# Differential attention: two partial row sums joined by TensorE in four column groups instead of by GpSimd

## The chip, the cores and the metric

The kernel runs on one core of a Trainium2 chip. The metric is the device time of one execution in microseconds; the time before is the median of 3 runs. The engines are TensorE (PE, its weight loads PEld), VectorE (DVE), ScalarE (ACT), GpSimd (POOL) and SyncE (SP), which issues the DMAs.

## What is computed

The program is a small model of two layers on an image of 2 x 256 channels x 48 x 48, so N = 2304 positions. Only the first layer's differential attention matters here. For each of 2 batches and 8 heads it computes, cut from the reference:

```python
Q1, Q2 = (Q[..., :hd], Q[..., hd:])          # hd = 32
K1, K2 = (K[..., :hd], K[..., hd:])
attn1 = softmax(einsum('bhnd,bhmd->bhnm', Q1, K1) * scale, axis=-1)
attn2 = softmax(einsum('bhnd,bhmd->bhnm', Q2, K2) * scale, axis=-1)
out = einsum('bhnm,bhmd->bhnd', attn1 - lam * attn2, V)
```

The kernel does not form the softmax: it exponentiates the scores less their row maximum, multiplies with V, and divides by the row sums of the exponentials at the end. The change is about these row sums, two (j = 0 and 1, for the two softmaxes) for each query.

## The kernel before, in words

`differential_attention` is the second of six stages. Its work is cut into 96 chunks (`CHUNKS`: 16 heads, 6 chunks of `WIDE` = 384 queries each). A chunk goes over 18 key tiles (`STEPS`) of 128 keys; for each tile and each j, TensorE makes 128 x 384 scores in a PSUM bank of a ring of four (`score`, line 417), and ScalarE writes their exponentials into one of nine `probs` buffers of 128 x 2 x 384 (`exps`, line 507). The keys lie on the partitions, so a row sum is a sum over the partitions and over the 18 tiles.

The tiles are first added up element by element, in two running sums: `on_dve` names the tiles 3, 7, 11 and 15, which VectorE adds (`add_up`, line 610, three additions, the last into `sum_dve`); the other 14 (`on_pool`) are added by GpSimd (line 661, 13 additions, into `run_pool`). Then GpSimd adds the two (line 667) into `row_sum`. Of these, TensorE makes the sum over the partitions in `sums(q)` (lines 458 to 465): a product with a matrix of ones for each j, the first in the upper half of the PSUM bank's partitions and the second in the lower. `s_accp` counts GpSimd's additions (`NPOOL` = 14 a chunk, with the joining one), `s_accd` VectorE's (`ND` = 3); `s_ring` counts the filled banks of the ring and `s_taken` the emptied ones.

From there the sums go by ScalarE to `sums_sb` (`take_sums`, line 528), by DMA to HBM and back in a compact form (`invert_sums`), through a reciprocal on VectorE (line 618), by DMA spread over the partitions, and into the product that normalises the output (line 626).

TensorE's order is written out by hand, in steps of three key tiles, six a chunk (`BATCHES`). A step consists of the six scores of the next three tiles, five products for the row maxima of a later chunk (line 428, reduced by VectorE in line 587, out of three PSUM banks), and the PV batch: the product of three tiles of `probs` with V (line 453, two halves of 64 columns, twelve recorded matmuls). After step 4 of a chunk's six (counted from 0) come the row maxima's broadcast (line 436), after the PV batch of step 1 the sums of the chunk before (`SUMS_AT`). VectorE takes the maxima of the same step, and after them an addition in the steps 1, 3 and 5, the reciprocal in step 2 and the normalising product in step 4. A `probs` buffer is written anew for the tile nine further on, when its PV product and its addition are done. All of these are f32.

Of the kernel before, what the change touches and what calls it, by code (L numbers as in the profile page):

```python
# [9 lines left out]
ALU = mybir.AluOpType  # L10
ACT = mybir.ActivationFunctionType
AX = mybir.AxisListType

P = 128
# [224 lines left out]
def differential_attention(nc, qk_hi, qk_lo, v_rows, lambdas, ident, row_sums, row_factors, o_rows):  # L239
# [18 lines left out]
    SUMS_AT, ROWS_AT, COMPACT_AT, NORMAL_AT = 1, 4, 2, 4  # L258
    PIECES = (0,), (1,), (2, 3), (4,)
    SCALE = HD ** -0.5  # L260
    on_dve = [g for g in range(STEPS) if g % 4 == 3]
    on_pool = [g for g in range(STEPS) if g not in on_dve]
    ND, NPOOL = len(on_dve) - 1, len(on_pool)
    add_after = {1: 1, 3: 2, 5: 3}
    TOTAL = CHUNKS * BATCHES

    def span(q):

        return q % PER_HEAD * T, T
# [34 lines left out]
    with ExitStack() as ctx:  # L304
# [2 lines left out]
        qs = [[sb(f"qs{i}{j}", [ROWS + 1, N], F32R) for j in range(2)] for i in range(2)]  # L307
        vs = [sb(f"vs{i}", [P, NT, 2, VD]) for i in range(2)]
        probs = [sb(f"probs{i}", [P, 2, WIDE]) for i in range(PBUF)]
        run_pool, row_sum, run_dve, sum_dve = (sb(n, [P, 2, WIDE]) for n in ("run_pool", "row_sum", "run_dve", "sum_dve"))  # L310
        maxes = [sb(f"maxes{i}", [P, 2, WIDE // P, PARTS_OF_KEYS]) for i in range(2)]
        neg_max = [sb(f"neg_max{i}", [P, 2, WIDE // P], F32R) for i in range(NEGS)]
        out_sb = sb("out", [P, WIDE])
        sums_sb = sb("sums", [P, WIDE])
        compact = sb("compact", [P, 2 * WIDE // P])
        compact_inv = sb("compact_inv", [P, 2 * WIDE // P])
        recip = sb("recip", [P, WIDE])
# [25 lines left out]
        with nc.Block() as block:  # L343
            @block.sync
            def _(sp):
                qh = qk_hi.rearrange("b (h j d) n -> (b h) j d n", j=2, d=HD)
                ql = qk_lo.rearrange("b (h j d) n -> (b h) j d n", j=2, d=HD)
                v_tiles = v_rows.rearrange("(t p) c -> p t c", p=P)

                def load(n, pieces):  # L350
                    par, (b, h) = n % 2, divmod(n, H0)
                    for piece in pieces:
                        if piece == 4:
                            sp.dma_start(vs[par][:, :, 0, :], v_tiles[:, b * NT:(b + 1) * NT, h * VD:(h + 1) * VD]
                                         ).then_inc(s_ldv[par], 16)
                        else:
                            j, kind = piece // 2, piece % 2
                            dst, parts = ((qs, (qh, qh, ql)), (ks, (qh, ql, qh)))[kind]
                            for r, src in enumerate(parts):
                                sp.dma_start(dst[par][j][r * HD:(r + 1) * HD, :].bitcast(F32),  # L360
                                             src[b * 2 * H0 + kind * H0 + h, j, :, :]).then_inc(s_ld[par], 16)

                def invert_sums(q):
                    w = span(q)[1]
                    sums_of, factors_of = row_sums[0:2 * w], row_factors[0:2 * w]
                    sp.wait_ge(s_taken, slot["sum", q] + 1)
                    sp.dma_start(sums_of.rearrange("(j n) -> j n", j=2), sums_sb[0:P:VD, 0:w]).then_inc(s_sums, 16)
                    sp.wait_ge(s_sums, (q + 1) * 16)
                    sp.dma_start(compact[:, 0:2 * w // P], sums_of.rearrange("(a c) -> a c", c=2 * w // P)
                                 ).then_inc(s_compact, 16)  # L370
                    sp.wait_ge(s_inv, q + 1)
                    sp.dma_start(factors_of.rearrange("(a c) -> a c", c=2 * w // P), compact_inv[:, 0:2 * w // P]
                                 ).then_inc(s_factors, 16)
                    sp.wait_ge(s_factors, (q + 1) * 16)
                    for j in range(2):
                        sp.dma_start(recip[j * VD:(j + 1) * VD, 0:w],
                                     factors_of[j * w:(j + 1) * w].partition_broadcast(VD)).then_inc(s_recip, 16)

                def store(q):
                    sp.wait_ge(s_norm, q + 1)  # L380
                    sp.dma_start(o_rows[:, q // PER_HEAD + 1, queries(q)], normed[:, 0:span(q)[1]]).then_inc(s_st_o, 16)

                sp.dma_start(ident_sb[:], ident).then_inc(s_const, 16)
                load(0, range(5))
                for i, l in enumerate(lambdas):
                    sp.dma_start(lam_in[:, i, :], l.rearrange("h d -> (h d)").partition_broadcast(P)).then_inc(s_lamin, 16)
                for q in range(CHUNKS):
                    n, c = divmod(q, PER_HEAD)
                    if q > 0:
                        invert_sums(q - 1)  # L390
                        store(q - 1)
                    if c < len(PIECES) and n + 1 < HEADS:

                        sp.wait_ge(s_pv, q * BATCHES + 1)
                        load(n + 1, PIECES[c])
                invert_sums(CHUNKS - 1)
                store(CHUNKS - 1)
                sp.wait_ge(s_st_o, CHUNKS * 16)

            @block.tensor  # L400
            def _(pe):
                pe.wait_ge(s_ones, 9)
                pe.wait_ge(s_ident, 1)

                def free(at):
# [50 lines left out]
                    mm.then_inc(s_pv, 1)  # L456

                def sums(q):
                    w = span(q)[1]
                    bank = free(slot["sum", q])  # L460
                    pe.wait_ge(s_accp, (q + 1) * NPOOL)
                    for j in range(2):
                        mm = pe.matmul(bank[VD * j:VD * (j + 1), 0:w], ones[:], row_sum[:, j, 0:w],
                                       start=True, stop=True, tile_position=(0, VD * j))
                    mm.then_inc(s_ring, 1)

                def scores_and_maxes(e, us):
# [25 lines left out]
            def _(act):  # L493
# [29 lines left out]
                def take_sums(q):  # L523
                    at = slot["sum", q]
                    if q > 0:
                        act.wait_ge(s_sums, q * 16)
                    act.wait_ge(s_ring, at + 1)
                    act.activation(sums_sb[:, 0:span(q)[1]], ring[at % BANKS][:, 0:span(q)[1]], ACT.Copy
                                   ).then_inc(s_taken, 1)

                act.wait_ge(s_lam, 2)
                act.activation(lam_exp[:], lam_sum[:], ACT.Exp).then_inc(s_lamexp, 1)
# [15 lines left out]
            def _(dve):  # L548
# [12 lines left out]
                def lambdas_ready():  # L561
                    dve.wait_ge(s_lamin, 16 * 4)
                    step = Chain(dve, s_lam)
                    for i in range(2):
                        ins = dve.tensor_tensor(lam_prod[:, i, :], lam_in[:, 2 * i, :], lam_in[:, 2 * i + 1, :], ALU.mult)
                    step.link(ins)
                    step.link(dve.tensor_reduce(lam_sum[:], lam_prod[:].rearrange("p i (h d) -> p i h d", d=HD),
                                                AX.X, ALU.add))
                    dve.wait_ge(s_lamexp, 1)
                    step.link(dve.tensor_tensor(lam_diff[:], lam_exp[:, 1, :], lam_exp[:, 0, :], ALU.subtract))  # L570
                    dve.wait_ge(s_ones, 9)
                    for b in range(B):
                        ins = dve.tensor_scalar(neg_lam[:, b * H0:(b + 1) * H0], lam_diff[:], -LAMBDA_INIT, None, ALU.add)
                    step.link(ins)
# [25 lines left out]
                def add_up(q, i):  # L600
# [3 lines left out]
                        dve.wait_ge(s_accd, q * ND + i - 1)  # L604
                    if i == ND and q > 0:

                        dve.wait_ge(s_accp, q * NPOOL)
                    acc = probs[on_dve[0] % PBUF] if i == 1 else run_dve
                    to = sum_dve if i == ND else run_dve
                    dve.tensor_tensor(to[:, :, 0:w], acc[:, :, 0:w], probs[g % PBUF][:, :, 0:w], ALU.add  # L610
# [37 lines left out]

            @block.gpsimd
            def _(pool):  # L650
                pool.memset(row_sum[:], 1.0).then_inc(s_ones, 1)
                for q in range(CHUNKS):
                    w = span(q)[1]
                    for i, g in enumerate(on_pool):
                        if i == 0:
                            continue
                        pool.wait_ge(s_taken, slot["score", q * STEPS + g, 1] + 1)
                        if q * NPOOL + i > 1:
                            pool.wait_ge(s_accp, q * NPOOL + i - 1)
                        acc = probs[on_pool[0] % PBUF] if i == 1 else run_pool  # L660
                        pool.tensor_tensor(run_pool[:, :, 0:w], acc[:, :, 0:w], probs[g % PBUF][:, :, 0:w], ALU.add  # L661
                                           ).then_inc(s_accp, 1)
                    pool.wait_ge(s_accd, (q + 1) * ND)
                    pool.wait_ge(s_accp, (q + 1) * NPOOL - 1)
                    if q > 0:
                        pool.wait_ge(s_ring, slot["sum", q - 1] + 1)
                    pool.tensor_tensor(row_sum[:, :, 0:w], run_pool[:, :, 0:w], sum_dve[:, :, 0:w], ALU.add  # L667
                                       ).then_inc(s_accp, 1)


def run_stages(eng, order, stage):
# [1535 lines left out]
```

## Time and profile before

| | us |
|---|---|
| median of 3 runs | 5432.79 (5431.19 to 5434.96) |
| the profiled execution | 5433.69 |
| its span | 5432.0 |
| TensorE busy in the span | 4963.1 |
| GpSimd busy in the span | 3056.2 |
| VectorE busy in the span | 3509.2 |

The span reaches from the first recorded instruction to the last. Busy times are sums over stages with different limits, so the stage in question has to be read by itself: it runs from 228 us, where its first DMA is issued, to about 3115 us, where the next stage begins. "Idle before" an instruction is the time that its engine did nothing just ahead of it, and the name behind an arrow is what ended that time. A matmul's recorded time contains its way through the array; what two of them cost is read from their starts.

### The profile page before, as it was taken

What the parts mean: (1) busy time and instruction counts of PE and PEld (TensorE: products, weight loads), DVE (VectorE), ACT (ScalarE), POOL (GpSimd) and SP (SyncE); (2) the same over time, 40 slices, a digit from 0 to 9 for tenths busy, and PEclk for the clock granted to TensorE, in tenths of its full rate; (3) what the DMA queues carried; (4) which work ended last, traced back from release to release, by engine and by line L of the source; (5) the groups of instructions that cost most, each with busy time, mean ns of one, the idle gap of its engine ahead of it and who ended that gap; (6) DMA issues with size and microseconds to landing.
All of it is one profiled execution on the core that took longest, in us unless ns stands there. A gap on an engine that the chain in (4) does not pass through costs nothing. (4 is left out here: it accounts for less than half of the span.)

```text
span 5432.0 us, 66178 instructions
## 1 busy us (share of the span) xinstructions
PE 4963.1 (91%) x22836; PEld 3030.5 (56%) x22836; DVE 3509.2 (65%) x5195; ACT 2424.0 (45%) x5309; POOL 3056.2 (56%) x1603
## 2 busy tenths in 40 slices
PE   8799999999999999999999779699996989888799
PEld 4465555555555555555555334377773555555355
DVE  3478887888878787888788445555553444545484
ACT  3255555555555555555555412144442333333332
POOL 0089999999999999999999711066661000000000
PEclk9899999999999999999999879799998999999899
DMA  6611111111111111111110056522201000000101
GB/s 221 209 42 40 33 32 45 41 32 40 38 45 32 33 40 45 40 33 32 45 41 18 25 155 174 159 56 71 71 14 63 24 16 14 23 17 12 52 7 53
DMA packets 229686, 295.77 MB, mean 54 GB/s; under 512 B 83326, under 2 KB 212870, under 8 KB 221838
## 3 DMA queue, kind: packets, MB, share of 16 engines
q1 hardware_dynamic: 229392, 292.06, 19.4%
q8 instruction: 159, 2.61, 0.2%
q14 instruction: 135, 1.11, 0.1%
HBM read 178.11 MB, written 113.87 MB: 54 GB/s over the span
## 5 line engine op out<-in xcount | busy, mean ns | idle before, releaser
L661 POOL TENSOR_TENSOR diff_run_pool<-diff_run_pool,diff_probs 128x768 f32<-128x768 f32 x1152 | 2233.4, 1939 | 170.9 <-ACT diff_probs L507 6.1
L587 DVE TENSOR_REDUCE diff_maxes<-diff_max 128x1 f32<-128x512 f32 (+1 forms) x2880 | 1627.9, 628 | 541.0 <-PE diff_max L428 540.6
L507 ACT ACTIVATE diff_probs<-diff_ring 128x384 f32<-128x384 f32 x3456 | 1432.9, 496 | 887.3 <-PE diff_ring L417 607.7
L453 PE MATMUL diff_out_ps<-diff_probs,diff_vs 128*64 128x384 f32 x6912 | 1245.3, 496 | 0.0
L428 PE MATMUL diff_max<-diff_ks,diff_qs 96*128 96x512 f32 (+1 forms) x2880 | 1146.2, 400 | 31.0 <-DMA diff_ks<-qk_hi 29.3
L417 PE MATMUL diff_ring<-diff_qs,diff_ks 97*128 97x384 f32 x3456 | 995.9, 343 | 47.8 <-ACT diff_probs L507 46.7
L428 PEld LDWEIGHTS diff_max<-diff_ks,diff_qs 96*128 96x128 f32 x2880 | 547.0, 190 | 397.2 <-issue 369.5
L417 PEld LDWEIGHTS diff_ring<-diff_qs,diff_ks 97*128 97x128 f32 x3456 | 654.3, 190 | 181.1 <-ACT diff_probs L507 85.1
L453 PEld LDWEIGHTS diff_out_ps<-diff_probs,diff_vs 128*64 128x64 f32 x6912 | 445.7, 136 | 513.4 <-issue 288.5
L2044 POOL MEMSET ffn_before<- 128x128 f32 x1 | 0.2, 204 | 988.5 <-POOLq L63 988.5
L1376 POOL TENSOR_TENSOR causal_run_sum<-causal_run_sum,causal_probs 128x768 f32<-128x768 f32 (+2 forms) x208 | 340.6, 1637 | 74.6 <-ACT causal_probs L1250 52.6
L1308 DVE TENSOR_REDUCE causal_maxes<-causal_max 128x2 f32<-128x768 f32 (+2 forms) x252 | 219.9, 873 | 248.0 <-PE causal_max L1183 164.8
L1250 ACT ACTIVATE causal_probs<-causal_ring 128x384 f32<-128x384 f32 (+2 forms) x504 | 206.2, 459 | 193.4 <-PE causal_ring L1161 105.7
L661 POOL TENSOR_TENSOR diff_run_pool<-diff_probs 128x768 f32<-128x768 f32 x96 | 222.8, 2321 | 54.9 <-ACT diff_probs L507 41.2
L610 DVE TENSOR_TENSOR diff_run_dve<-diff_probs 128x768 f32<-128x768 f32 x96 | 234.3, 2441 | 10.5 <-ACT diff_probs L507 10.5
L1182 PE MATMUL causal_max<-causal_ka,causal_qa 128*128 128x384 f32 (+2 forms) x504 | 177.7, 353 | 35.6 <-DVE causal_ident_r L1302 34.4
L982 POOL TENSOR_TENSOR mid_o_in<-mid_o_one,mid_o_two 128x1536 f32<-128x1536 f32 x12 | 41.1, 3428 | 261.2 <-DMA mid_o_two<-o_rows 224.9
L1160 PE MATMUL causal_ring<-causal_qa,causal_ka 128*128 128x384 f32 (+2 forms) x504 | 182.2, 362 | 0.9 <-ACT causal_probs L1250 0.9
L667 POOL TENSOR_TENSOR diff_row_sum<-diff_run_pool,diff_sum_dve 128x768 f32<-128x768 f32 x96 | 174.4, 1817 | 14.3 <-DVE diff_sum_dve L610 1.7
L1719 DVE RECIPROCAL rec_rstd<-rec_std 128x384 f32<-128x384 f32 x36 | 91.9, 2553 | 118.7 <-ACT rec_std L1642 118.7
L1183 PE MATMUL causal_max<-causal_kb,causal_qb 96*128 96x384 f32 (+2 forms) x504 | 165.9, 329 | 0.0
L1207 PE MATMUL causal_out_ps<-causal_probs,causal_vs 128*64 128x384 f32 (+2 forms) x1008 | 165.5, 464 | 0.0
(229 smaller groups left out, 5940.5 us busy)
## 6 DMA issues: line engine op xcount, KB each, us to landing
qk_hi<-proj_hi SPq DMA_DIRECT2D x12, 1536.0 KB, 5.8
qk_lo<-proj_lo SPq DMA_DIRECT2D x12, 1536.0 KB, 9.6
diff_qs<-qk_hi SPq DMA_DIRECT2D x64, 288.0 KB, 4.4
diff_ks<-qk_hi SPq DMA_DIRECT2D x64, 288.0 KB, 6.0
diff_recip<-row_factors SPq DMA_DIRECT2D x192, 96.0 KB, 2.8
o_rows<-diff_normed SPq DMA_DIRECT2D x96, 192.0 KB, 1.9
v_rows<-proj_vst SPq DMA_DIRECT2D x12, 768.0 KB, 7.6
diff_qs<-qk_lo SPq DMA_DIRECT2D x32, 288.0 KB, 5.3
```

What stands on the lines that cost most here:

```text
L417: pe.matmul(bank[:, 0:span(q)[1]], ks[par][j][:, g * P:(g + 1) * P], qs[par][j][:, queries(q)], start=True, stop=True).then_inc(s_ring, 1)
L428: pe.matmul(max_ps[u % MAX_BANKS][:, 0:keys.stop - keys.start], qs[n % 2][j][0:ROWS, at:at + P], ks[n % 2][j][0:ROWS, keys], start=True, s ...
L453: mm = pe.matmul(out_ps[VD * j:VD * (j + 1), 0:w], vs[n % 2][:, g, j, :], probs[g % PBUF][:, j, 0:w], start=g == 0, stop=g == STEPS - 1, t ...
L507: act.activation(probs[g % PBUF][:, j, 0:w], ring[at % BANKS][:, 0:w], ACT.Exp, scale=SCALE).then_inc(s_taken, 1)
L587: dve.tensor_reduce(maxes[q % 2][:, j, s:s + 1, h], max_ps[u % MAX_BANKS][:, 0:w], AX.X, ALU.max).then_inc(s_red, 1)
L610: dve.tensor_tensor(to[:, :, 0:w], acc[:, :, 0:w], probs[g % PBUF][:, :, 0:w], ALU.add).then_inc(s_accd, 1)
L661: pool.tensor_tensor(run_pool[:, :, 0:w], acc[:, :, 0:w], probs[g % PBUF][:, :, 0:w], ALU.add).then_inc(s_accp, 1)
L1160: pe.matmul(bank[:, lo:T], ka[turn % 2][j][:, keys], qa[j][:, queries], start=True, stop=False)
L1182: pe.matmul(to[:, j, 0:n], qa[j][:, queries], ka[turn % 2][j][:, keys], start=True, stop=False)
L1250: act.activation(probs[tile % PBUF][:, j, lo:T], ring[at % BANKS][:, lo:T], ACT.Exp, scale=SCALE).then_inc(s_taken, 1)
L1308: dve.tensor_reduce(maxes[z % 2][:, :, s, k], max_ps[u % 2][:, :, 0:n], AX.X, ALU.max).then_inc(s_red, 1)
L1376: pool.tensor_tensor(acc[:, :, lo:T], acc[:, :, lo:T], probs[tile % PBUF][:, :, lo:T], ALU.add).then_inc(s_acc, 1)
```

## The change

GpSimd's joining addition is given up, with the tile `row_sum` and its memset. GpSimd's last addition writes `sum_pool` instead of `run_pool`, as VectorE's last writes `sum_dve`. TensorE's `sums(q)` takes both: for each of the two partial sums, each j and each half of the 384 queries it makes a product of 192 columns with a ones matrix of 32 columns, eight products in all; the four (j, half) go to four groups of 32 partitions of the same bank, and the second partial sum is accumulated onto the first. The bank then holds 192 columns in place of 384, and the copy to `sums_sb` and the DMA out of it change accordingly. TensorE waits for VectorE's last addition itself, and VectorE and GpSimd wait, before they write their partial sums again, for the sums of the chunk before.

```diff
-    ND, NPOOL = len(on_dve) - 1, len(on_pool)
+    ND, NPOOL = len(on_dve) - 1, len(on_pool) - 1
...
-                    sp.dma_start(sums_of.rearrange("(j n) -> j n", j=2), sums_sb[0:P:VD, 0:w]).then_inc(s_sums, 16)
+                    sp.dma_start(sums_of.rearrange("(r n) -> r n", r=P // QUAD), sums_sb[0:P:QUAD, 0:w // 2]
+                                 ).then_inc(s_sums, 16)
...
                 def sums(q):
-                    w = span(q)[1]
+                    w = span(q)[1] // 2
                     bank = free(slot["sum", q])
                     pe.wait_ge(s_accp, (q + 1) * NPOOL)
-                    for j in range(2):
-                        mm = pe.matmul(bank[VD * j:VD * (j + 1), 0:w], ones[:], row_sum[:, j, 0:w],
-                                       start=True, stop=True, tile_position=(0, VD * j))
+                    pe.wait_ge(s_accd, (q + 1) * ND)
+                    for part in (sum_pool, sum_dve):
+                        for j in range(2):
+                            for half in range(2):
+                                row = (2 * j + half) * QUAD
+                                mm = pe.matmul(bank[row:row + QUAD, 0:w], ones[:, 0:QUAD],
+                                               part[:, j, half * w:(half + 1) * w], start=part is sum_pool,
+                                               stop=part is sum_dve, tile_position=(0, row))
                     mm.then_inc(s_ring, 1)
...
-                    act.activation(sums_sb[:, 0:span(q)[1]], ring[at % BANKS][:, 0:span(q)[1]], ACT.Copy
-                                   ).then_inc(s_taken, 1)
+                    w = span(q)[1] // 2
+                    act.activation(sums_sb[:, 0:w], ring[at % BANKS][:, 0:w], ACT.Copy).then_inc(s_taken, 1)
...
                     if i == ND and q > 0:
 
-                        dve.wait_ge(s_accp, q * NPOOL)
+                        dve.wait_ge(s_ring, slot["sum", q - 1] + 1)
...
-                pool.memset(row_sum[:], 1.0).then_inc(s_ones, 1)
...
+                        if i == NPOOL and q > 0:
+
+                            pool.wait_ge(s_ring, slot["sum", q - 1] + 1)
                         acc = probs[on_pool[0] % PBUF] if i == 1 else run_pool
-                        pool.tensor_tensor(run_pool[:, :, 0:w], acc[:, :, 0:w], probs[g % PBUF][:, :, 0:w], ALU.add
+                        to = sum_pool if i == NPOOL else run_pool
+                        pool.tensor_tensor(to[:, :, 0:w], acc[:, :, 0:w], probs[g % PBUF][:, :, 0:w], ALU.add
                                            ).then_inc(s_accp, 1)
-                    pool.wait_ge(s_accd, (q + 1) * ND)
-                    pool.wait_ge(s_accp, (q + 1) * NPOOL - 1)
-                    if q > 0:
-                        pool.wait_ge(s_ring, slot["sum", q - 1] + 1)
-                    pool.tensor_tensor(row_sum[:, :, 0:w], run_pool[:, :, 0:w], sum_dve[:, :, 0:w], ALU.add
-                                       ).then_inc(s_accp, 1)
```

## Rows read from the trace of the kernel before

**Rows 1.** The page: GpSimd's busy tenths in 40 equal slices of the span.

```profile
POOL 0089999999999999999999711066661000000000
```

**Rows 2.** Groups of GpSimd's instructions, 500 to 3099 us: count, busy, mean ns, idle before.

```profile
L661 POOL TENSOR_TENSOR diff_run_pool<-diff_run_pool,diff_probs 128x768 f32<-128x768 f32 x1061 | 2054.6, 1937 | 152.1
L661 POOL TENSOR_TENSOR diff_run_pool<-diff_probs 128x768 f32<-128x768 f32 x88 | 207.7, 2360 | 12.6
L667 POOL TENSOR_TENSOR diff_row_sum<-diff_run_pool,diff_sum_dve 128x768 f32<-128x768 f32 x89 | 161.6, 1816 | 11.8
```

**Rows 3.** Who waited for whom, 504 to 3099 us: us in total, times, longest.

```profile
ACT diff_probs L507 <- POOL diff_run_pool L661: 85.9, 87, 1.3
...
PE diff_ring L463 <- POOL diff_row_sum L667: 59.5, 86, 2.2
PE diff_ring L417 <- ACT diff_probs L507: 46.4, 88, 0.8
```

**Rows 4.** TensorE in order of time, settled chunk: start us, us, [idle before <-releaser].

```profile
2009.01 2.16 PE L453 MATMUL diff_out_ps<-diff_probs,diff_vs 128*64 128x384 f32 x12
2011.85 0.87 PE L463 MATMUL diff_ring<-diff_row_sum,diff_ones 128*64 128x384 f32 x4 [0.68 <-POOL diff_row_sum L667]
...
2015.74 2.16 PE L453 MATMUL diff_out_ps<-diff_probs,diff_vs 128*64 128x384 f32 x12
```

**Rows 5.** TensorE in order of time, early chunks: their PV batches, sums, one wait.

```profile
306.43 2.16 PE L453 MATMUL diff_out_ps<-diff_probs,diff_vs 128*64 128x384 f32 x12
...
334.13 2.16 PE L453 MATMUL diff_out_ps<-diff_probs,diff_vs 128*64 128x384 f32 x12
...
338.53 2.16 PE L453 MATMUL diff_out_ps<-diff_probs,diff_vs 128*64 128x384 f32 x12
340.51 0.81 PE L463 MATMUL diff_ring<-diff_row_sum,diff_ones 128*64 128x384 f32 x4
...
343.60 2.16 PE L453 MATMUL diff_out_ps<-diff_probs,diff_vs 128*64 128x384 f32 x12
...
361.62 0.50 PE L428 MATMUL diff_max<-diff_ks,diff_qs 96*128 96x512 f32 x1 [0.22 <-DVE diff_maxes L587]
...
362.53 2.16 PE L453 MATMUL diff_out_ps<-diff_probs,diff_vs 128*64 128x384 f32 x12
...
476.06 2.16 PE L453 MATMUL diff_out_ps<-diff_probs,diff_vs 128*64 128x384 f32 x12
```

**Rows 6.** Line 667, the joins: count, duration ns min/median/max, first and last start.

```profile
L667 POOL TENSOR_TENSOR diff_row_sum<-diff_run_pool,diff_sum_dve x96: 1799/1811/2347, 304.0 to 3097.7; 128x768 f32<-128x768 f32 x96
```

**Rows 7.** TensorE's weight loads in order of time, end of a settled PV batch.

```profile
2001.24 0.14 PEld L453 LDWEIGHTS diff_out_ps<-diff_probs,diff_vs 128*64 128x64 f32 x2 [0.18 <-ACT diff_probs L507]
2001.57 0.14 PEld L453 LDWEIGHTS diff_out_ps<-diff_probs,diff_vs 128*64 128x64 f32 x2 [0.18 <-issue]
2002.31 0.19 PEld L428 LDWEIGHTS diff_max<-diff_ks,diff_qs 96*128 96x128 f32 x1 [0.60 <-issue]
```

**Rows 8.** The same view, first stage, f32 products of 512 columns, full width.

```profile
151.02 0.19 PEld L167 LDWEIGHTS proj_v<-proj_wv,proj_xn 128*128 128x128 f32 x1 [0.24 <-issue]
151.45 0.19 PEld L167 LDWEIGHTS proj_v<-proj_wv,proj_xn 128*128 128x128 f32 x1 [0.24 <-issue]
```

**Rows 9.** Line 610, VectorE's first and last additions of a chunk: as rows 6.

```profile
L610 DVE TENSOR_TENSOR diff_run_dve<-diff_probs x96: 947/2539/2601, 284.7 to 3067.6; 128x768 f32<-128x768 f32 x96
...
L610 DVE TENSOR_TENSOR diff_sum_dve<-diff_run_dve,diff_probs x96: 945/947/2583, 303.0 to 3084.3; 128x768 f32<-128x768 f32 x96
```

**Rows 10.** Line 661, GpSimd's additions: as rows 6.

```profile
L661 POOL TENSOR_TENSOR diff_run_pool<-diff_run_pool,diff_probs x1152: 1798/1828/2488, 272.0 to 3095.8; 128x768 f32<-128x768 f32 x192
L661 POOL TENSOR_TENSOR diff_run_pool<-diff_probs x96: 1809/2367/2371, 270.1 to 3071.2; 128x768 f32<-128x768 f32 x96
```

**Rows 11.** TensorE in order of time, last chunk: first PV batch, and the sums.

```profile
3062.42 2.16 PE L453 MATMUL diff_out_ps<-diff_probs,diff_vs 128*64 128x384 f32 x12
...
3099.68 1.55 PE L463 MATMUL diff_ring<-diff_row_sum,diff_ones 128*64 128x384 f32 x4 [10.91 <-POOL diff_row_sum L667]
```

More of the change, by code:

```diff
@@ L260, in differential_attention @@
     SCALE = HD ** -0.5
+    QUAD = 32
     on_dve = [g for g in range(STEPS) if g % 4 == 3]
     on_pool = [g for g in range(STEPS) if g not in on_dve]
-    ND, NPOOL = len(on_dve) - 1, len(on_pool)
+    ND, NPOOL = len(on_dve) - 1, len(on_pool) - 1
     add_after = {1: 1, 3: 2, 5: 3}
@@ L309, in differential_attention @@
         probs = [sb(f"probs{i}", [P, 2, WIDE]) for i in range(PBUF)]
-        run_pool, row_sum, run_dve, sum_dve = (sb(n, [P, 2, WIDE]) for n in ("run_pool", "row_sum", "run_dve", "sum_dve"))
+        run_pool, sum_pool, run_dve, sum_dve = (sb(n, [P, 2, WIDE]) for n in ("run_pool", "sum_pool", "run_dve", "sum_dve"))
         maxes = [sb(f"maxes{i}", [P, 2, WIDE // P, PARTS_OF_KEYS]) for i in range(2)]
@@ L313, in differential_attention @@
         out_sb = sb("out", [P, WIDE])
-        sums_sb = sb("sums", [P, WIDE])
+        sums_sb = sb("sums", [P, WIDE // 2])
         compact = sb("compact", [P, 2 * WIDE // P])
@@ L401, in _ @@
             def _(pe):
-                pe.wait_ge(s_ones, 9)
+                pe.wait_ge(s_ones, 8)
                 pe.wait_ge(s_ident, 1)
@@ L570, in lambdas_ready @@
                     step.link(dve.tensor_tensor(lam_diff[:], lam_exp[:, 1, :], lam_exp[:, 0, :], ALU.subtract))
-                    dve.wait_ge(s_ones, 9)
+                    dve.wait_ge(s_ones, 8)
                     for b in range(B):
```

## Prediction, made before the result was known

> **What bounds the kernel now.** I read the page first, for where GpSimd (POOL) is busy, then POOL's groups of instructions over the settled part of the differential stage, the list of waits there, and last TensorE's order of time, once in a settled query chunk and once in an early one. The change lies wholly in this stage, 96 chunks long; nothing outside it is touched.
>
> In the page's slices POOL stands at eight or nine tenths from the third slice to the twenty-third [rows 1]. The groups say that this is saturation: between 500 and 3099 us the three groups are busy 2054.6, 207.7 and 161.6 us and idle 152.1, 12.6 and 11.8 us before their instructions, together 2600 us for a stretch of 2599 us. The idle time is 0.143 us for each of 1238 instructions, with no releaser named: the engine's own step from one addition to the next, not a wait [rows 2]. So a chunk lasts as long as its 13 additions and the joining one: (3097.7 - 304.0) / 95 = 29.41 us [rows 6].
>
> TensorE is paced by this through two waits a chunk: the sums wait for the join (59.5 us in 86 times), and a score waits for ScalarE (46.4 us), which itself waits for a probs buffer that POOL has not yet added (85.9 us) [rows 3]. Both fall into one step of TensorE's six. In the settled chunk it takes 6.73 us from one PV batch to the next, 2009.01 to 2015.74 [rows 4]; the same step of an early chunk, where POOL's backlog is still small and the sums start without a wait, takes 5.07 us, 338.53 to 343.60 [rows 5]. The early stretch shows what TensorE does if POOL lets it: 27.70 us for the chunk from 306.43 to 334.13, 28.40 for the next (to 362.53), and (476.06 - 306.43) / 6 = 28.27 on average [rows 5]. This, 1.14 us under 29.41, is where a shorter POOL chain can lead, and not POOL's own saving of 1.96 us.
>
> **POOL loses the join.** It takes 1.816 us and its step 0.14 [rows 2]: 1.96 us a chunk. POOL's own need falls to 29.41 - 1.96 = 27.45 us. Its last addition now writes sum_pool instead of run_pool; the join, of the same shape and also to a third tile, ran no longer than the others (1.816 against 1.937 us on average), so I cost this at nothing, between -0.1 and +0.1 us. The two tests of `s_ring` that guard the partial sums, on POOL's last addition and on VectorE's (in place of `s_accp`), ask for the sums of the chunk before, done four steps earlier; the cover is some 15 us of other additions, and without it POOL and VectorE would stall until TensorE's step 1. The memset that goes ran ahead of the stage's first loads: nothing.
>
> **TensorE's sums change shape.** Before: two f32 products of 384 columns, recorded as four matmuls, two in each half of the array. The pairs are worth seeing: weight loads of the PV batch come two at a time, 0.32 us apart (2001.24, 2001.57) [rows 7], while in the first stage f32 matmuls over the full width come singly, 0.43 us apart for 512 columns, which is 0.32 for 384 [rows 8]. So the halves run side by side, and the sums take 2 x 0.32 = 0.64 us; the step with them is 5.07 us against a plain one of (27.70 - 2 x 5.07) / 4 = 4.39 (the step with the row maxima, the other long one, taken as equal), a difference of 0.68 [rows 5]. After: eight products of 192 columns, so sixteen matmuls of 0.16 us, in four groups of 32 columns. No row shows more than two groups at once. If all four run side by side, it is 4 x 0.16 = 0.64 us again; two at a time, 1.29; one at a time, 2.58. I take four, as the halves show no loss against the full width [rows 7, 8]. To this comes one more change of shape, from 64-column groups to 32: the last pair's matmul starts 0.32 us after its load at 2001.57, the next full-width load at 2002.31, 0.42 us later, thus 0.1 us over the 0.32 that it streams [rows 7]. New price 0.74 us, so TensorE's floor becomes 27.70 + 0.1 = 27.80 us; ends of the unknown -0.1 and +2.0.
>
> The Trainium skill (TensorE: Matmul & The Clock Gate, Measured speedup vs the span model) gives 2.38 times for three column groups, which is 79% of three. By that the four rounds would be some 0.81 us, an estimate, and the sum below 16 us smaller; no row here can tell.
>
> The added wait of TensorE for `s_accd` asks for an addition that ended a step before (POOL's join waited for it until now): nothing, and behind it would stand the next step's maxima. ScalarE's copy of 192 instead of 384 columns is shorter, the DMA of the sums has four rows of 768 bytes instead of two of 1536, and both lie under the next step's work; nothing, with 0 to +0.1 us for the chain of DMAs, which VectorE's reciprocal meets sooner.
>
> **What is late next.** With 27.45 against 27.80 us POOL is no longer the bound, but barely, so VectorE's collisions with it become visible. VectorE's additions take 0.95 us alone, yet 2.5 in the median of the first of a chunk and up to 2.6 of the last [rows 9], and POOL's go from 1.83 to 2.37 when they meet one [rows 10]: each waits until the other has ended. In the settled kernel this hides behind POOL's queue. In the early chunk it does not: the maxima follow late, TensorE waits for VectorE at 361.62, and the chunk is 0.70 us longer than the one before [rows 5]. The six early chunks carry 28.27 - 27.70 = 0.57 us of such stalls each. With POOL nearly caught up its first addition begins shortly before VectorE's last one wants the same port in every chunk, which I expect to cost 0.3 to 0.6 us; I take 0.5, so a chunk of 27.80 + 0.5 = 28.3 us.
>
> **The end of the stage.** In the last chunk TensorE ends its PV batches early and then stands 10.91 us for POOL's backlog; the sums start at 3099.68, 37.3 us after the chunk's first PV batch (3062.42) [rows 11]. Without backlog POOL's 13 additions, 13 x (1.83 + 0.14) = 25.6 us and 1 us of collisions, begin about 3 us ahead of that batch (an estimate: the second tile is scored a step earlier): 24 us, so 13 us less.
>
> **Sum.** From the first PV batch of the second chunk to that of the last were 3062.42 - 306.43 = 2756.0 us, 94 chunks of 29.32 [rows 5, 11]. 94 x 28.3 = 2660.2: 95.8 less, and 13 at the end: 109 us. The span of 5432.0 becomes 5323; the profiled execution took 1.7 us more than its span (5433.69) and 0.9 more than the median (5432.79), so I say 5324 us.
>
> **Rivals.** (a) *Two groups at a time*, or sixteen pairs of load and matmul that cannot be issued faster: 0.65 us more a chunk, 28.95: 94 x 0.37 + 13 = 48 us less, 5385. Against it stands that the halves lose nothing; for it that four streams were never tried.
>
> (b) *One group at a time, slower than before.* Sums of 2.58 + 0.1 instead of 0.68 put 2.0 us on TensorE's path: 29.70 without any collision, 30.3 with them. Between 36 - 13 = 23 and 92 - 13 = 79 us more; 5480 as the middle. It decides from a chunk of 29.32 + 13 / 94 = 29.46 us on, that is, from sums of 1.9 us with the collisions counted. The rows speak against it: the loads of one pair lie inside the streaming of the pair before, in all 128 rows [rows 7]. The Trainium skill (TensorE: Matmul & The Clock Gate, The mechanism) says that a weight load overlaps a running matmul only where the row group differs; here all groups have the same rows, and by that rule this rival would hold. The trace disagrees, with loads 0.32 us apart beside matmuls that stream 0.32 us.
>
> (c) *Collisions at two steps of every chunk* with 0.7 us each: 27.8 + 1.4 = 29.2, hence 11 + 13 = 24 us less, 5408. For it: three VectorE additions and one product a chunk meet a POOL that is 98% busy. Against it: the early chunks, as busy, averaged 0.57.
>
> (d) *The other side of the forecast*: POOL locks to the steps so that no addition collides, 27.9: 5286.
>
> **Chances.** Forecast 0.67 (its own range 5285 to 5355, chunks of 27.9 to 28.6 us), (a) 0.15, (b) 0.05, (c) 0.09, (d) 0.04. What a measurement of this kernel can tell from no change is some 0.2%, 11 us. The forecast, (a), (d) and most of (c) are faster by more: 0.92; the rest of (c) 0.03 the same; (b) 0.05 slower. The range 5284 to 5393 holds the forecast, (a) and half of (d).
>
> **What would show it.** POOL: 13 additions a chunk and gaps over 0.2 us, waiting for ScalarE. TensorE: no wait for POOL ahead of the sums; 16 matmuls in about 0.7 us, four starting together (if two by two, (a); spread over 2.5 us, (b)); step with sums near 5.15 us. A step longer by 0.3 to 0.7 us with TensorE waiting for VectorE's maxima would be the collisions; two of them a chunk, (c). The sums of the last chunk some 24 us after its first PV batch. The forecast is wrong if TensorE's chunk has another floor than 27.8 us, or POOL is still without gaps.

## The result and the profile after

The changed kernel takes 5338.88 us (median of 4 runs, 5333.89 to 5341.33), against 5433.88 us of the kernel before in the same sessions: 95 us less, a ratio of 0.9823 with a 95% interval from 0.9806 to 0.984. The profiled execution took 5341.33 us, its span 5339.6.

GpSimd is no longer full. The page's slices, to be laid beside [rows 1]:

```profile
POOL 0089889889899889988888511166670000000000
```

And GpSimd's groups from 500 to 3000 us (count, busy us, mean ns, idle before and what ended it), to be laid beside [rows 2]:

```profile
L671 POOL TENSOR_TENSOR diff_run_pool<-diff_run_pool,diff_probs 128x768 f32<-128x768 f32 x968 | 1925.5, 1989 | 211.5 <-ACT diff_probs L514 95.4 <-POOL diff_run_pool L671 3.5 <-ACT diff_qs L521 0.4
L671 POOL TENSOR_TENSOR diff_sum_pool<-diff_run_pool,diff_probs 128x768 f32<-128x768 f32 x87 | 162.6, 1869 | 12.1 <-issue 0.8
L671 POOL TENSOR_TENSOR diff_run_pool<-diff_probs 128x768 f32<-128x768 f32 x88 | 159.7, 1814 | 29.9 <-ACT diff_probs L514 20.3
```

The joining addition is gone, and the idle time now names a releaser: GpSimd waits for ScalarE's exponentials, 95.4 + 20.3 = 115.7 us in 88 chunks, 1.3 us a chunk. The whole list of waits counts 198 of them:

```profile
POOL diff_run_pool L671 <- ACT diff_probs L514: 115.7, 198, 1.1
DVE diff_compact_inv L625 <- DMA diff_compact<-row_sums: 60.7, 88, 4.3
```

Before, no wait of GpSimd's was named in [rows 2]. The second line, VectorE's reciprocal waiting for the DMA of the sums, is taken up below.

TensorE in order of time, from the last step of one chunk to the second of the next (start us, us, engine, line, operation), beside [rows 4, 5]:

```profile
1495.06 2.16 PE L455 MATMUL diff_out_ps<-diff_probs,diff_vs 128*64 128x384 f32 x12
...
1499.90 2.16 PE L455 MATMUL diff_out_ps<-diff_probs,diff_vs 128*64 128x384 f32 x12
...
1504.30 2.16 PE L455 MATMUL diff_out_ps<-diff_probs,diff_vs 128*64 128x384 f32 x12
1506.38 0.53 PE L469 MATMUL diff_ring<-diff_sum_pool,diff_ones 128*32 128x192 f32 x8
1506.73 0.51 PE L469 MATMUL diff_ring<-diff_sum_dve,diff_ones 128*32 128x192 f32 x8
1507.17 0.50 PE L430 MATMUL diff_max<-diff_ks,diff_qs 96*128 96x512 f32 x1
...
1509.49 2.16 PE L455 MATMUL diff_out_ps<-diff_probs,diff_vs 128*64 128x384 f32 x12
```

The step with the sums takes 1509.49 - 1504.30 = 5.19 us, without a wait ahead of the sums; in the settled kernel before it took 6.73 [rows 4]. The plain step from 1499.90 takes 4.40 us. The step across the chunk's border, 1495.06 to 1499.90, takes 4.84, which is 0.44 us too much; the experiments are about this. The new shape of the sums costs what was taken for it: the first eight matmuls are 0.35 us ahead of the next eight, so a round of four column groups takes 0.17 us.

TensorE's weight loads at the same place show the same (start us, us):

```profile
1506.38 0.16 PEld L469 LDWEIGHTS diff_ring<-diff_sum_pool,diff_ones 128*32 128x32 f32 x8 [0.60 <-issue]
1506.57 0.29 PEld L469 LDWEIGHTS diff_ring<-diff_sum_dve,diff_ones 128*32 128x32 f32 x8
```

Eight loads within 0.16 us, and eight more beside the matmuls that stream; with one group at a time, as in rival (b), they would have been spread over 2.6 us.

The end of the stage, beside [rows 11], TensorE's first PV batch of the last chunk and its sums:

```profile
2978.01 2.16 PE L455 MATMUL diff_out_ps<-diff_probs,diff_vs 128*64 128x384 f32 x12
...
3003.07 0.87 PE L469 MATMUL diff_ring<-diff_sum_pool,diff_ones 128*32 128x192 f32 x8 [4.41 <-issue]
```

So the last sums start 3099.68 - 3003.07 = 96.6 us earlier. This splits into 94 chunks of (2978.01 - 304.92) / 94 = 28.44 us in place of 29.32, which is 83 us (304.92 is the first PV batch of the second chunk, 306.43 before [rows 5]: 1.5 us); and an end of 25.1 us in place of 37.3, 12 us. The span is shorter by 92.4 us only; by the first and last instructions of each stage, most of the difference lies in the second attention stage, which the change does not touch: 617.0 us in the profile before, 619.9 in this one. In the profiles below it is 616.8 to 617.1 in four and 619.9 in three, so it does not follow the edits.

### The profile page after: what moved, and what is told of

It is laid out like the page before. It is cut to its first block and busy times, and to the rows that moved or that the text cites. A ratio compares the mean times of both kernels' runs of the same rounds, so it can differ in the third digit from the quotient of the medians.

```text
span 5339.6 us, 68289 instructions
## 1 busy us (share of the span) xinstructions
PE 4968.2 (93%) x23988; PEld 3051.7 (57%) x23988; DVE 3456.5 (65%) x5195; ACT 2365.5 (44%) x5309; POOL 2878.0 (54%) x1506
## 5 line engine op out<-in xcount | busy, mean ns | idle before, releaser
L671 POOL TENSOR_TENSOR diff_run_pool<-diff_run_pool,diff_probs 128x768 f32<-128x768 f32 x1056 | 2099.6, 1988 | 233.7 <-ACT diff_probs L514 107.2
L514 ACT ACTIVATE diff_probs<-diff_ring 128x384 f32<-128x384 f32 x3456 | 1389.4, 508 | 846.8 <-PE diff_ring L419 805.0
L430 PE MATMUL diff_max<-diff_ks,diff_qs 96*128 96x512 f32 (+1 forms) x2880 | 1164.5, 406 | 42.1 <-DMA diff_ks<-qk_hi 29.4
L671 POOL TENSOR_TENSOR diff_run_pool<-diff_probs 128x768 f32<-128x768 f32 x96 | 174.2, 1814 | 302.3 <-ACT diff_probs L514 292.0
L617 DVE TENSOR_TENSOR diff_sum_dve<-diff_run_dve,diff_probs 128x768 f32<-128x768 f32 x96 | 212.8, 2217 | 0.0
L671 POOL TENSOR_TENSOR diff_sum_pool<-diff_run_pool,diff_probs 128x768 f32<-128x768 f32 x96 | 179.4, 1869 | 13.3 <-issue 0.8
L1165 PE MATMUL causal_ring<-causal_qb,causal_kb 97*128 97x384 f32 (+2 forms) x504 | 166.1, 330 | 0.0
```

The costliest lines, as they stand in the source:

```text
L430: pe.matmul(max_ps[u % MAX_BANKS][:, 0:keys.stop - keys.start], qs[n % 2][j][0:ROWS, at:at + P], ks[n % 2][j][0:ROWS, keys], start=True, s ...
L514: act.activation(probs[g % PBUF][:, j, 0:w], ring[at % BANKS][:, 0:w], ACT.Exp, scale=SCALE).then_inc(s_taken, 1)
L671: pool.tensor_tensor(to[:, :, 0:w], acc[:, :, 0:w], probs[g % PBUF][:, :, 0:w], ALU.add).then_inc(s_accp, 1)
```

## The experiments

Each kernel is the changed one with the edit shown. The ratios are to the kernel before as it ran beside each of them (medians 5432.98 us for e1 to e4, 5434.04 for e5 to e7). The mean chunk is read from the first PV batches of the second chunk and of the last, 94 chunks apart.

| kernel | median us | ratio to before (95%) | these two batches, us | mean chunk, us |
|---|---|---|---|---|
| before | 5433.88 | | 306.43, 3062.42 | 29.32 |
| changed | 5338.88 | 0.9823 (0.9806 to 0.9840) | 304.92, 2978.01 | 28.44 |
| e1, idle join | 5422.74 | 0.9983 (0.9973 to 0.9992) | 305.33, 3053.90 | 29.24 |
| e2, two groups | 5386.27 | 0.9918 (0.9901 to 0.9934) | 305.29, 3025.42 | 28.94 |
| e3, third addition later | 5310.41 | 0.9776 (0.9760 to 0.9792) | 304.26, 2946.05 | 28.10 |
| e4, scaling earlier | 5327.95 | 0.9810 (0.9794 to 0.9826) | 303.25, 2965.81 | 28.33 |
| e5, half the idle join | 5347.27 | 0.9839 (0.9823 to 0.9855) | 306.18, 2987.69 | 28.53 |
| e6, first addition waits | 5297.08 | 0.9750 (0.9733 to 0.9766) | 304.52, 2938.06 | 28.02 |
| e7, e6 with e4 | 5280.69 | 0.9718 (0.9701 to 0.9734) | 306.21, 2926.53 | 27.88 |

**e1. Was it GpSimd's time, or TensorE's wait for its result?** An addition of the join's shape comes back, and nobody reads it.

```diff
-    ND, NPOOL = len(on_dve) - 1, len(on_pool) - 1
+    ND, NPOOL = len(on_dve) - 1, len(on_pool)
...
-                    pe.wait_ge(s_accp, (q + 1) * NPOOL)
+                    pe.wait_ge(s_accp, (q + 1) * NPOOL - 1)
...
+                    pool.wait_ge(s_accp, (q + 1) * NPOOL - 1)
+                    pool.tensor_tensor(extra[:, :, 0:w], run_pool[:, :, 0:w], sum_pool[:, :, 0:w], ALU.add
+                                       ).then_inc(s_accp, 1)
```

> The changed kernel, with one GpSimd addition of the join's shape put back at the end of each chunk (run_pool + sum_pool into a tile that nobody reads); TensorE does not wait for it and sums as in the changed kernel. Theory (GpSimd's chain of additions was the bound): GpSimd needs 27.45 + 1.96 = 29.4 us a chunk again, is without gaps, and the time goes back to about 5430 us (before: 5433.9); TensorE again meets waits through ScalarE for probs buffers. Rival (what cost time was TensorE's wait for the join's result, not GpSimd's time): nobody waits for this addition, so the chunk stays near the changed kernel's 28.44 us and the time near 5339 us.

It goes back to 5422.74 us, with a chunk of 29.24. GpSimd's groups from 500 to 3050 us, and one line of its list of waits (us in total, times, longest):

```profile
L671 POOL TENSOR_TENSOR diff_run_pool<-diff_run_pool,diff_probs 128x768 f32<-128x768 f32 x956 | 1865.7, 1952 | 139.2 <-POOL diff_run_pool L671 1.7 <-ACT diff_probs L514 1.3
L671 POOL TENSOR_TENSOR diff_run_pool<-diff_probs 128x768 f32<-128x768 f32 x87 | 196.3, 2257 | 12.5
L674 POOL TENSOR_TENSOR diff_extra<-diff_run_pool,diff_sum_pool 128x768 f32<-128x768 f32 x87 | 159.9, 1838 | 6.8
L671 POOL TENSOR_TENSOR diff_sum_pool<-diff_run_pool,diff_probs 128x768 f32<-128x768 f32 x87 | 158.9, 1827 | 11.8 <-ACT diff_probs L514 0.4
```

```profile
ACT diff_probs L514 <- POOL diff_run_pool L671: 117.2, 65, 2.3
```

GpSimd is without gaps again, and what it holds up is now ScalarE, which waits for probs buffers, as the theory said: the time belongs to GpSimd's chain, and who reads the last link hardly matters. It ends 10 us under the kernel before, not 4 as expected; 94 x 0.08 = 8 us of this are in the chunks, the rest in the last one, where the idle addition holds up nobody.

**e2. Is TensorE's own work now what a chunk lasts?** The same sums, made in two column groups of 384 columns instead of four of 192. The tile `sums_sb`, the copy into it and the DMA out of it take their shapes of before again; of the edit only the products are shown.

```diff
                     for part in (sum_pool, sum_dve):
                         for j in range(2):
-                            for half in range(2):
-                                row = (2 * j + half) * QUAD
-                                mm = pe.matmul(bank[row:row + QUAD, 0:w], ones[:, 0:QUAD],
-                                               part[:, j, half * w:(half + 1) * w], start=part is sum_pool,
-                                               stop=part is sum_dve, tile_position=(0, row))
+                            mm = pe.matmul(bank[VD * j:VD * (j + 1), 0:w], ones[:], part[:, j, 0:w],
+                                           start=part is sum_pool, stop=part is sum_dve, tile_position=(0, VD * j))
```

> The changed kernel, with the two partial sums summed by TensorE in two column groups of 64 and 384 columns each, as the single sum was before, in place of four groups of 32 and 192 columns. Theory (TensorE's own work is now the bound, and groups run side by side): the sums cost 4 x 0.32 = 1.29 us instead of 0.80, less 0.1 for the change of shape that falls away is already in the 0.80; the step with the sums goes from 5.19 to about 5.68 us, the chunk from 28.44 to 28.9 us, the time from 5339 to about 5385 us. Rival (the chunk is set by GpSimd and VectorE with their collisions, TensorE has slack): the step grows, but another one shrinks, and the time stays within 10 us of 5339.

TensorE in order of time:

```profile
1526.38 2.16 PE L454 MATMUL diff_out_ps<-diff_probs,diff_vs 128*64 128x384 f32 x12
1528.36 0.81 PE L466 MATMUL diff_ring<-diff_sum_pool,diff_ones 128*64 128x384 f32 x4
1529.01 0.81 PE L466 MATMUL diff_ring<-diff_sum_dve,diff_ones 128*64 128x384 f32 x4
...
1532.07 2.16 PE L454 MATMUL diff_out_ps<-diff_probs,diff_vs 128*64 128x384 f32 x12
```

The step is 5.69 us long, 0.50 more than with four groups, the chunk is longer by 28.94 - 28.44 = 0.50, and the time by 47 us. All of TensorE's time shows. This is also what the prediction's rival (a) would have given, 5385 us: four groups in place of two are worth 47 us here, half of what the whole change brings.

**e3 and e6. What are the 0.44 us at the chunk's border?** The profile after shows VectorE's third addition of the chunk there. Two views of the changed kernel in order of time, GpSimd's and VectorE's:

```profile
1495.70 1.81 POOL L671 TENSOR_TENSOR diff_run_pool<-diff_probs 128x768 f32<-128x768 f32 x1
1497.66 10.78 POOL L671 TENSOR_TENSOR diff_run_pool<-diff_run_pool,diff_probs 128x768 f32<-128x768 f32 x5
```

```profile
1496.03 2.30 DVE L617 TENSOR_TENSOR diff_sum_dve<-diff_run_dve,diff_probs 128x768 f32<-128x768 f32 x1
1498.26 2.80 DVE L594 TENSOR_REDUCE diff_maxes<-diff_max 128x1 f32<-128x512 f32 x5
```

GpSimd's first addition of the new chunk starts 0.33 us ahead of VectorE's last of the old one. VectorE's ends 2.30 us after its start, 0.82 us after GpSimd's has ended at 1497.51, though it takes 0.95 alone; the maxima, which begin behind it, are late, and TensorE's fourth and fifth products for the maxima wait for a bank, as the weight load of the fourth shows:

```profile
1498.99 0.19 PEld L430 LDWEIGHTS diff_max<-diff_ks,diff_qs 96*128 96x128 f32 x1 [0.30 <-DVE diff_maxes L594]
```

To tell this from a VectorE that is simply too full at this step, one run moves VectorE's addition, and another leaves VectorE alone and makes GpSimd's first addition start later, by the order of its tiles.

```diff
-    add_after = {1: 1, 3: 2, 5: 3}
+    add_after = {1: 1, 3: 2}
...
+                    if b == 0 and q > 0:
+                        add_up(q - 1, ND)
...
+                add_up(CHUNKS - 1, ND)
                 invert(CHUNKS - 1)
```

> The changed kernel, with VectorE's third addition of a chunk moved from step 5 to step 0 of the next chunk (one step before the sums that need it). Theory (the 0.44 us by which the step to the next chunk's first PV batch exceeds 4.39 is this addition, held up by GpSimd's first addition of the chunk, so that the maxima come late): that step goes to 4.39 us, the chunk from 28.29 to about 27.85 us (29.0 to 28.6 in every sixth), the time from 5339 to about 5298 us. Rival 1 (GpSimd's need, 27.45 us and the arrival of its tiles, holds the chunk at 28.3): the 0.44 us turns up elsewhere as a wait for probs buffers, 5339 us. Rival 2 (the addition collides in step 0 as well): the stall moves one step, 5339 us.

```diff
-    on_pool = [g for g in range(STEPS) if g not in on_dve]
+    on_pool = [0, 2, 1] + [g for g in range(3, STEPS) if g not in on_dve]
```

> The changed kernel, with GpSimd taking the first three tiles of a chunk in the order 0, 2, 1: its first addition then has to wait for tile 2 and starts 0.4 to 0.8 us later, after VectorE's third addition of the chunk before has begun. Nothing else is changed; VectorE's order and work are the same. Theory (the 0.44 us of stall comes from VectorE's third addition standing behind GpSimd's first, 0.3 us after its start): the third addition takes 0.95 us instead of 2.3, GpSimd's first 2.37 instead of 1.81, the step to the next chunk's first PV batch goes from 4.84 to 4.39 us, the chunk to 27.85 us, the time from 5339 to about 5300 us. Rival (VectorE is too full at step 5 whatever GpSimd does): third addition or maxima as late as before, 5339 us. Rival 2 (GpSimd loses 0.8 us a chunk and has no room for it): the chunk stays at 28.3 us with waits for probs buffers.

In e6, with the one changed list, GpSimd and VectorE in order of time:

```profile
1477.78 2.62 POOL L671 TENSOR_TENSOR diff_run_pool<-diff_probs 128x768 f32<-128x768 f32 x1 [0.37 <-ACT diff_probs L514]
```

```profile
1477.77 0.95 DVE L617 TENSOR_TENSOR diff_sum_dve<-diff_run_dve,diff_probs 128x768 f32<-128x768 f32 x1
```

VectorE is now 0.01 us ahead and done in 0.95 us, and it is GpSimd that takes 2.62. Over the stage, line 617's third addition in the changed kernel and in e6 (count, ns min/median/max, first and last start, forms):

```profile
L617 DVE TENSOR_TENSOR diff_sum_dve<-diff_run_dve,diff_probs x96: 1872/2295/2592, 301.3 to 2994.9; 128x768 f32<-128x768 f32 x96
```

```profile
L617 DVE TENSOR_TENSOR diff_sum_dve<-diff_run_dve,diff_probs x96: 945/948/2573, 301.1 to 2955.0; 128x768 f32<-128x768 f32 x96
```

And TensorE's step across the border, e6:

```profile
1472.41 2.16 PE L455 MATMUL diff_out_ps<-diff_probs,diff_vs 128*64 128x384 f32 x12
...
1476.81 2.16 PE L455 MATMUL diff_out_ps<-diff_probs,diff_vs 128*64 128x384 f32 x12
```

It is back at 4.40 us, and the time falls by 42 us to 5297.08: the stall is the collision, since VectorE does the same work in the same order as before. GpSimd loses 0.8 us in the same place, and nothing comes of it at this step, because it has some 1.0 us to spare (below). In e3 the border step is plain as well (the mean over chunks 9 to 94 falls from 4.75 to 4.39 us) and the chunk falls to 28.10; the addition still takes 1.87 us in the median, but in a step with room for it. Its time, 5310, lies 12 over the expected 5298: I had taken the 0.44 us off every chunk, while every sixth did not have them (next run), so that the mean is 0.36. That is 94 x 0.08 = 8 of the 12 us; the other 4 are not taken apart.

**e4. What is late in every sixth chunk?** It lasts 29.0 us instead of 28.29. VectorE in order of time there, and the product for the maxima on TensorE that waits:

```profile
1454.90 0.19 DVE L625 RECIPROCAL diff_compact_inv<-diff_compact 128x6 f32<-128x6 f32 x1 [1.67 <-DMA diff_compact<-row_sums]
1455.01 1.04 DVE L587 TENSOR_SCALAR diff_vs<-diff_vs,diff_neg_lam 128x1152 f32<-128x1152 f32 x1
1455.97 2.80 DVE L594 TENSOR_REDUCE diff_maxes<-diff_max 128x1 f32<-128x512 f32 x5
```

```profile
1456.70 0.50 PE L430 MATMUL diff_max<-diff_ks,diff_qs 96*128 96x512 f32 x1 [0.56 <-DVE diff_maxes L594]
```

The scaling of the values stands behind the reciprocal, which stands behind the DMA of the sums. But this chunk, with a wait of 1.67 us for the DMA, is one of four such among the fifteen (1.35 to 1.99 us). In the other eleven the reciprocal waits 0.36 to 0.78 us, and the scaling itself takes 1.9 to 2.3 us, where its shortest is 0.80. One of them, VectorE and GpSimd in order of time:

```profile
1623.99 0.19 DVE L625 RECIPROCAL diff_compact_inv<-diff_compact 128x6 f32<-128x6 f32 x1 [0.36 <-DMA diff_compact<-row_sums]
1624.09 2.34 DVE L587 TENSOR_SCALAR diff_vs<-diff_vs,diff_neg_lam 128x1152 f32<-128x1152 f32 x1
```

```profile
1623.99 1.82 POOL L671 TENSOR_TENSOR diff_run_pool<-diff_run_pool,diff_probs 128x768 f32<-128x768 f32 x1
```

GpSimd's addition starts 0.10 us ahead, and the scaling ends 0.62 us after it: a second collision of the kind that e6 shows. In e6, where GpSimd's additions stand elsewhere in the chunk, the scaling keeps its place and the same chunk reads:

```profile
1603.56 0.19 DVE L625 RECIPROCAL diff_compact_inv<-diff_compact 128x6 f32<-128x6 f32 x1 [0.34 <-DMA diff_compact<-row_sums]
1603.67 1.12 DVE L587 TENSOR_SCALAR diff_vs<-diff_vs,diff_neg_lam 128x1152 f32<-128x1152 f32 x1
```

The DMA is as late, the scaling is done in 1.12 us, and ten of e6's fifteen such chunks last 27.84 to 27.89 us, an eleventh 28.02. The other four, which have the longest waits for the DMA, 1.35 to 1.74 us, last 31.3 (three) and 29.6. So the sixth chunk is late mostly by the collision, and in four of fifteen the DMA is late as well; why in these is not shown. The run of e4 moves the scaling away from the DMA and from that addition at once, so it does not tell the two apart.

```diff
-                    if b == COMPACT_AT and (q + 1) % PER_HEAD == 0 and q + 1 < CHUNKS:
+                    if b == 0 and (q + 1) % PER_HEAD == 0 and q + 1 < CHUNKS:
```

> The changed kernel, with the scaling of the next head's values (16 times in all, on VectorE) moved from step 2 to step 0 of the same chunk. Theory (in every sixth chunk the scaling, which takes 2.3 us beside GpSimd and 0.8 alone, and stands behind a reciprocal that waits for a DMA, delays the maxima of step 3: 5.41 instead of 4.39 us): step 3 goes back to 4.39 and the sixth chunk from 29.0 to about 28.3 us, 16 x 0.7 = 11 us less, about 5328 us. Rival (the same delay in the step after, 0): no change, 5339 us.

5327.95 us, as expected to the microsecond. Not every sixth chunk is repaired: 12 of the 15 that can be read lie between 28.2 and 28.6 us, the other three at 28.97, 28.97 and 29.17; these are the ones with the longest waits for the DMA, 1.93 to 2.08 us.

**e5. How much room has GpSimd?** As e1, with half the columns in the idle addition.

```diff
-                    pool.tensor_tensor(extra[:, :, 0:w], run_pool[:, :, 0:w], sum_pool[:, :, 0:w], ALU.add
+                    pool.tensor_tensor(extra[:, 0, 0:w], run_pool[:, 0, 0:w], sum_pool[:, 0, 0:w], ALU.add
```

> As the run with the idle joining addition, but with half its elements (1 x 384 instead of 2 x 384 columns): a GpSimd addition of some 1.1 us a chunk with its step, read by nobody. Theory (GpSimd waits some 1.3 us a chunk for tiles in the changed kernel, so this much more fits in): the chunk stays between 28.3 and 28.6 us, the time within 15 us of the changed kernel's 5339. Rival (GpSimd is still the bound, or the collisions grow in step with its work): the chunk grows by the 1.1 us, to 29.3 us and 5420 us.

The time is 5347.27 us, within the 15 us, but for reasons that I had only half right. Its group, 500 to 2960 us:

```profile
L674 POOL TENSOR_TENSOR diff_extra<-diff_run_pool,diff_sum_pool 128x384 f32<-128x384 f32 x87 | 139.5, 1604 | 6.8
```

It takes 1.60 us where I had put 1.0 (its shortest is 1.00), because it is now the one that meets VectorE's third addition, which starts 0.25 us ahead of it. GpSimd's waits for tiles are used up (1.7 us in 4 times), the chunk is 28.53, and GpSimd is at its limit again. The step across the border is 4.40 us here, but the one with the row maxima, plain at 5.07, is 5.70 in the median: the collision has moved to VectorE's second addition (2.25 us in the median, 0.96 in the changed kernel).

**e7. Both edits together.** The list of e6 and the line of e4.

> The run before together with the earlier scaling of the values (step 0 instead of step 2, 16 times). Theory: both stalls are gone, every chunk lasts the sum of TensorE's steps, 4 x 4.39 + 5.07 + 5.19 = 27.82 us, the mean 27.9; against the changed kernel's 28.44 that is 94 x 0.54 = 51 us less, about 5288 us. Rival (the two edits get in each other's way at step 0): about 5300 us, as with the order of the tiles alone.

5280.69 us, the fastest version, 2.8% under the kernel before, 58 us under the changed one and 7 under the 5288 expected. Its waits that touch VectorE's maxima, 500 to 2930 us, and for comparison the same lines of the changed kernel, 500 to 3000 us:

```profile
PEld diff_max L430 <- DVE diff_maxes L594: 5.4, 16, 0.9
PE diff_max L430 <- DVE diff_maxes L594: 0.8, 2, 0.6
```

```profile
PEld diff_max L430 <- DVE diff_maxes L594: 68.9, 195, 1.0
PE diff_max L430 <- DVE diff_maxes L594: 11.2, 22, 0.7
```

TensorE's waits for VectorE have gone from 80 us to 6, and the mean chunk, 27.88 us, is the sum of TensorE's steps: 4 x 4.39 + 5.07 + 5.19 = 27.82. What is left of this stage is TensorE's own work.

## Why the prediction was right, step by step

Forecast 5324, measured 5339: 95 us less, in place of 109. The forecast's own case held, and most of the difference lies in the size of one term.

**The bound.** Right: GpSimd's saturation set the chunk. e1 shows that 1.8 us of its work that nobody reads costs 84 us, and that the dependency as such is worth 10 at most.

**TensorE's sums.** Right, with a small error. Put at 0.74 us, they are 5.19 - 4.39 = 0.80; the floor is 27.82 us instead of 27.80. That four groups run as well as two was inferred from the halves; rival (b), one group at a time, is out by the loads above, and rival (a) is what e2 shows, 47 us dearer (I had 61). The rule that a weight load overlaps a running matmul only in another row group (the Trainium skill, TensorE: Matmul & The Clock Gate, section The mechanism) does not hold for these column groups, which all use the same 128 rows and whose second eight loads run beside the matmuls; the same section also allows a load ahead into a background weight buffer, and no run here tells whether that is the way. Nor is there the loss that I estimated from the 2.38 times for three groups (the Trainium skill, TensorE: Matmul & The Clock Gate, section Measured speedup vs the span model), 0.81 us for four rounds: two rounds take 0.35 us, so four take 0.70.

**What is late next.** The mechanism was right to the instruction: GpSimd's first addition begins "shortly before VectorE's last one wants the same port in every chunk", 0.33 us before. The term was mis-sized. I took 0.5 us of stalls a chunk; they are 28.44 - 27.82 = 0.62. The collision itself, 0.44 us in five chunks of six, was within the 0.3 to 0.6 that I gave it. What I had not priced by itself is the sixth chunk, whose excess is 29.0 - 27.82 = 1.2 us: mostly GpSimd's collision with the scaling, and in four of fifteen also the wait for the DMA of the sums that I had put at 0 to 0.1 us. VectorE's reciprocal now waits 60.7 us in 88 times, 0.69 each; in e7, where no scaling stands behind it, it still waits 56.7 us in 87 times, and the mean chunk is the sum of TensorE's steps but for 0.06 us. 94 x 0.14 us for chunks of 28.44 instead of 28.3 are 13 us, and 3 of the other microseconds lie in stages that the change does not touch.

**GpSimd's need.** Right: put at 27.45 us, it is 27.4. Its 13 additions take 2247.8 us in 2500, which is 25.57 a chunk and as much as before (25.60 [rows 2]): the first addition no longer collides (1.81 us instead of 2.36), but the middle ones are longer (1.99 instead of 1.94). To this come 13 steps of 0.143 us. The room is then 28.44 - 27.4 = 1.0 us; the waits for tiles add up to 1.3 because each of the 198 contains such a step. Barely not the bound, as said: e5 uses the room up.

**The end of the stage.** Put at 24 us, 13 less; it is 25.1, 12 less.

**The chances.** Rival (c), two collisions of 0.7 us in every chunk, did not come true, and (d), none at all, neither; but e6 and e7 come out near where (d) was put, at 5297 and 5281 us against 5286: one list away, and for e7 one more line. The additions still collide there, only it is GpSimd that waits (2.62 us).

## What to carry to other kernels

Find the engine whose idle gaps name no releaser over the whole stage; what is taken from it counts until the next engine's floor, and here that floor could be read in the same trace, from an early stretch in which the queue had not yet built up. Where GpSimd's additions share a stage with VectorE's, look at who starts first: here, once neither was hidden behind a full queue, the order of one engine's operands was worth 42 us beside the 95 of the change itself. And before a late instruction is put down to what it waits for, look at its own duration too: in most of the sixth chunks the wait for the DMA was short and the scaling itself was long. And a sum over the partitions can take over a joining addition in PSUM at little cost, if the product is spread over enough column groups: 0.80 us a chunk of TensorE's time here in place of 0.68.

## What was not expected of the hardware

Four column groups of 32 columns with f32 operands run side by side with next to no loss: a round of four takes 0.17 us, where 192 columns are 0.16 us by the 0.32 us of 384 [rows 7]. The 16 matmuls of 192 columns lengthen the step by 0.80 us, with the changes of shape, against 5.69 - 4.39 = 1.30 in two groups of 64 with 384 columns. And the price of a collision depends on who comes first. With GpSimd 0.33 us ahead, VectorE's addition takes 2.30 us instead of 0.95 and GpSimd's is undisturbed at 1.81; with VectorE 0.01 us ahead, VectorE's takes 0.95 and GpSimd's 2.62. The first order cost this kernel 0.44 us in five chunks of six, the second nothing at that step.
